# Block-quantised MLP of a two-layer decoder: down projection from float32r halves, split over two steps, block maxima kept in a PSUM bank

## The reference

```python
def _mx_dequant(t):                      # blocks of 32 along the last dim
    blocks = t.reshape(rows, feat // _BLOCK, _BLOCK)
    max_abs = jnp.max(jnp.abs(blocks), axis=-1)
    scales = jnp.maximum(max_abs / _FP8_MAX, _EPS)
    q = (blocks / scales[..., None]).astype(jnp.float8_e4m3fn).astype(jnp.float32)
    return (q * scales[..., None]).reshape(rows, feat)

def _mx_linear(x2d, w):
    return _mx_dequant(x2d) @ _mx_dequant(w).T
...
gate = _mx_linear(x2d, gate_w)
up = _mx_linear(x2d, up_w)
...
out = _mx_linear(h, down_w)
...
x = x + _L1_ffn_ref(_layernorm(x, axis=-1), L1_ffn_gate_w, L1_ffn_up_w, L1_ffn_down_w)
```

## Time and profile before

| | us |
|---|---|
| median of 3 runs | 1530.81 |
| the profiled execution | 1529.1 |
| its span in the profile | 1527.0 |
| TensorE busy | 1450.7 (95%) |
| VectorE busy | 1117.6 (73%) |
| ScalarE busy | 978.1 (64%) |
| GpSimd busy | 730.9 (48%) |
| the last stage, first projection to the end of the span | 1348.0 to 1527.0 |

### The profile page before, as it was taken

How to read it: one execution, slowest core, us unless ns; L and a number is a source line. 1 busy time by engine, 2 the same in 40 slices (tenths; PEclk the granted TensorE clock), 3 DMA queues, 4 the chain that set the end, 5 groups by cost and what they waited for, 6 DMA issues and landing times. The chain is left out here.

```text
span 1527.0 us, 30711 instructions
## 1 busy us (share of the span) xinstructions
PE 1450.7 (95%) x10384; PEld 1201.9 (79%) x10384; DVE 1117.6 (73%) x2544; ACT 978.1 (64%) x2620; POOL 730.9 (48%) x894
## 2 busy tenths in 40 slices
PE   5999899999999999899998999899999999889998
PEld 3676578888888888688874555489999999867887
DVE  5888678888888887554446777656777777788887
ACT  2787577777778777433336888677877777742222
POOL 3766545555555555232323343113444444457765
PEclk9999999999999999999999999999999999999999
DMA  6000010000000000000002000120000000000000
GB/s 255 2 2 2 29 69 3 5 3 5 3 3 5 4 3 1 24 1 1 1 20 119 2 1 2 33 80 8 8 8 9 8 2 2 1 1 15 14 11 18
DMA packets 15611, 29.84 MB, mean 20 GB/s; under 512 B 1505, under 2 KB 12002, under 8 KB 14690
## 3 DMA queue, kind: packets, MB, share of 16 engines
q1 hardware_dynamic: 15458, 27.89, 5.0%
HBM read 25.79 MB, written 2.10 MB: 18 GB/s over the span
## 5 line engine op out<-in xcount | busy, mean ns | idle before, releaser
L1517 POOL TENSOR_TENSOR weights_even<-weights_even,cross_reciprocal 128x512 f32<-128x512 f32 x64 | 66.6, 1040 | 189.1 <-DVE cross_reciprocal L1771 189.1
L962 POOL TENSOR_TENSOR cross_work<-cross_work,cross_reciprocal 128x512 f32<-128x512 f32 x64 | 66.6, 1040 | 175.2 <-DVE cross_reciprocal L1130 175.2
L1208 PE MATMUL bank<-ident,cross_work 128*128 128x128 f32 x768 | 116.9, 275 | 1.4 <-DVE cross_work L1108 1.1
L1015 ACT ACTIVATE cross_work<-bank,cross_shift,cross_q_rms 128x128 f32<-128x128 f32 x256 | 113.6, 455 | 4.5 <-DVE cross_shift L1102 3.5
L1208 PEld LDWEIGHTS bank<-ident,cross_work 128*128 128x128 f32 x768 | 89.5, 140 | 29.0 <-DVE cross_work L1108 20.5
L2062 POOL TENSOR_TENSOR mlp_low_inner<-mlp_inner,mlp_high_inner 128x512 fp32r<-128x512 f32 x35 | 47.5, 1356 | 114.5 <-ACT mlp_high_inner L2106 114.5
L2598 DVE TENSOR_REDUCE grouped_maxima<-bank 128x4 bf16<-128x512 f32 x128 | 82.3, 684 | 25.5 <-PE bank L2690 25.5
L1606 ACT ACTIVATE weights_even<-bank,cross_shift 128x128 f32<-128x128 f32 x256 | 90.4, 366 | 13.0 <-DVE cross_shift L1763 12.0
L1761 DVE TENSOR_REDUCE cross_maxima<-bank 128x4 f32<-128x512 f32 x64 | 44.1, 689 | 69.6 <-PE bank L1909 69.6
L2962 ACT ACTIVATE mx_silu<-bank 128x512 f32<-128x512 f32 x32 | 19.1, 598 | 113.4 <-PE bank L3112 113.3
L411 POOL TENSOR_TENSOR causal_masked_maxima<-causal_maxima,causal_constants 128x512 bf16<-128x512 bf16 x64 | 66.5, 1061 | 45.0 <-DVE causal_maxima L562 40.7
(11 more groups left out here) (388 smaller groups left out, 5357.4 us busy)
## 6 DMA issues: line engine op xcount, KB each, us to landing
weights_even<-in_weights SPq DMA_DIRECT2D x2, 2560.0 KB, 12.4
weights_even<-in_weights SPq DMA_DIRECT2D x2, 1732.0 KB, 9.6
weights_odd_early<-in_weights SPq DMA_DIRECT2D x1, 3072.0 KB, 11.8
weights_odd_values<-in_weights SPq DMA_DIRECT2D x1, 3072.0 KB, 18.9
weights_odd_late<-in_weights SPq DMA_DIRECT2D x2, 1536.0 KB, 9.5
x<-in_x SPq DMA_DIRECT2D x4, 512.0 KB, 8.2
out<-mx_result SPq DMA_DIRECT2D x16, 128.0 KB, 1.7
weights_even<-in_weights SPq DMA_DIRECT2D x2, 512.0 KB, 6.1
```

The costliest lines, as they stand in the source:

```text
L962: pool.tensor_tensor(probs[x], probs[x], reciprocal[x][:, :].unsqueeze(2).to_broadcast([P, PER, P]), ALU.mult).then_inc(probs_divided, 1)
L1015: last = act.activation(probs[x][:, j, :], bank_scores[:, j * P:(j + 1) * P], ACT.Exp, scale=q_rms[x][:, j:j + 1], bias=shift[x][:, j:j + ...
L1208: last = pe.transpose(bank[:, j * P:(j + 1) * P], source, core.ident[:, :])
L1517: pool.tensor_tensor(probs[x], probs[x], reciprocal[x][:, :].unsqueeze(2).to_broadcast([P, JOBS, P]), ALU.mult).then_inc(probs_divided, 1)
```

## The change

The down projection is made of float32r halves, as the up projection was already: `innerT` and the down weights each become a high and a low tensor, and for each tile three products of 128x256 are made (high with high weights, high with low weights, low with high weights), 24 for a batch. The high part of the transposed inner half is ScalarE's copy, as before, now with float32r out. The low part is new work of VectorE: `make_low_innerT`, PSUM minus high part, 128x512, one for each half, placed between `gate` and `scale_inner`. The low down weights are made once by GpSimd, four subtractions of 128x512 between the roundings of batch 0 (`low_down_weights`); ScalarE writes the high ones with four more copies.

Half 0 of a batch's down projection stays at its place at the end of step b+2 (`down_half(t - 2, 0)`). Half 1 is made one step later, behind the first projection of step b+3. So `bank_y` is complete one piece later, and `add_to_x` of batch t-3 moves behind `scale_inner` of half 0.

`largest` of the inner scaling is the first 16 columns of the bank of the up projection, which is free once `gate` has read it.

```diff
-        self.largest, self.scale, self.inverse = (layer.sbuf(f"{name}_{x}", [P, blocks])
-                                                  for x in ("largest", "scale", "inverse"))
+        self.largest = layer.sbuf(f"{name}_largest", [P, blocks]) if largest is None else largest
...
-        scratch = [Scratch(layer, f"inner{j}", INTER // HALVES) for j in range(HALVES)]
+        banks_of_up = [core.banks[2], core.banks[4]]
+        scratch = [Scratch(layer, f"inner{j}", INTER // HALVES, largest=banks_of_up[j][:, 0:INTER // HALVES // BLOCK])
+                   for j in range(HALVES)]
...
+            def low_down_weights(jobs):
+                for k in jobs:
+                    pool.wait_ge(weights_ready, GATE_UP_JOBS - TURNED_EARLY + k + 1)
+                    tiles = slice(2 * k, 2 * k + 2)
+                    pool.tensor_tensor(down_split[1][:, tiles, :], w_down[:, tiles, :],
+                                       down_split[0][:, tiles, :].bitcast(F32), ALU.subtract).then_inc(down_low, 1)
...
+                    if isinstance(b, int) and b == 0:
+                        low_down_weights((2 * j, 2 * j + 1))
...
+                        act.activation(down_split[0][:, m:m + 2, :].rearrange("p i n -> p (i n)"),
+                                       bank_turn[k % 2][:, :], ACT.Copy)
...
+            def make_low_innerT(b, j):
+                dve.wait_ge(innerT_high, HALVES * b + j + 1)
+                dve.tensor_tensor(innerT[1][:, 4 * j:4 * j + 4, :], bank_turn[j].rearrange("p (i t) -> p i t", i=4),
+                                  innerT[0][:, 4 * j:4 * j + 4, :].bitcast(F32), ALU.subtract).then_inc(innerT_low, 1)
...
-                if batch_there(t - 3) and t - 3 != VERY_LAST - 1:
+                if batch_there(t - 3) and not batch_there(t - 1) and t - 3 != VERY_LAST - 1:
                     add_to_x(t - 3, 1 - s)
...
                         if j == 1 and batch_there(t):
                             make_low(t)
+                        if batch_there(t - 2):
+                            make_low_innerT(t - 2, j)
                         scale_inner(i, j)
+                        if j == 0 and batch_there(t - 3):
+                            add_to_x(t - 3, 1 - s)
...
+            WITH_HIGH, WITH_LOW = ((0, 0), (0, 1)), ((1, 0),)
+
+            def down_half(b, j):
+                if j == 0:
+                    pe.wait_ge(result_ready, nonneg(b))
+                if isinstance(b, int) and b == 0:
+                    pe.wait_ge(down_low, (j + 1) * (WEIGHT_JOBS - GATE_UP_JOBS) // HALVES)
+                tiles = range(4 * j, 4 * j + 4)
+                pe.wait_ge(innerT_high, HALVES * b + j + 1)
+                down_products(tiles, WITH_HIGH, first=(j == 0))
+                pe.wait_ge(innerT_low, HALVES * b + j + 1)
+                product = down_products(tiles, WITH_LOW, last=(j == HALVES - 1))
+                if j == HALVES - 1:
+                    product.then_inc(layer.y_filled, 1)
...
                     if batch_there(t - 1):
                         project(t - 1, j)
+                    if j == 0 and batch_there(t - 3) and t - 3 != VERY_LAST:
+                        down_half(t - 3, 1)
                     if batch_there(t - 2):
                         turn_inner(t - 2, s, j)
...
-                    down(t - 2)
+                    down_half(t - 2, 0)
```

More of the change, by code:

```diff
@@ L2860, in mx_mlp @@
         inner_q = [sbuf(f"inner_q{s}", [P, INTER]) for s in range(2)]
-        innerT = sbuf("innerT", [P, TILES, P])
+        innerT = [sbuf(f"{half}_innerT", [P, TILES, P], F32R) for half in ("high", "low")]
+        down_split = [sbuf(f"{half}_down", [P, TILES, EMBED], F32R) for half in ("high", "low")]
         result = [sbuf(f"result{s}", [P, EMBED]) for s in range(2)]
         bank_h, bank_turn, bank_y = core.banks[0], core.banks[5:7], core.banks[7]
-        bank_gate, bank_up = [core.banks[1], core.banks[3]], [core.banks[2], core.banks[4]]
+        bank_gate, bank_up = [core.banks[1], core.banks[3]], banks_of_up
         weight_banks = [core.banks[k] for k in (5, 6, 7, 3)]
@@ L2991, in step @@
                     if batch_there(t - 2) and (t - 2, j) != (VERY_LAST, 1):
-                        copy_innerT(t - 2, j)
+                        copy_high_innerT(t - 2, j)
                 if t - 2 == VERY_LAST:
@@ L3084, in step @@
                     make_low(t)
+                if t - 2 == VERY_LAST:
+                    make_low_innerT(VERY_LAST, 0)
+                    for k in range(PIECES):
+                        make_low_last_piece(k)
             batches(dve, step)
@@ L3129, in turn_h, with down_products @@
                 last.then_inc(layer.hT_filled, 1)
-            def down(b):
-                pe.wait_ge(result_ready, nonneg(b))
-                for m in range(TILES):
-                    if m % 4 == 0:
-                        pe.wait_ge(innerT_ready, HALVES * b + m // 4 + 1)
-                    last = pe.matmul(bank_y[:, 0:EMBED], innerT[:, m, :], w_down[:, m, :],
-                                     start=(m == 0), stop=(m == TILES - 1))
-                last.then_inc(layer.y_filled, 1)
-            def down_tiles(tiles):
-                for m in tiles:
-                    last = pe.matmul(bank_y[:, 0:EMBED], innerT[:, m, :], w_down[:, m, :],
-                                     start=(m == 0), stop=(m == TILES - 1))
-                return last
+            def down_products(tiles, parts, first=False, last=False):
+                jobs = [(m, a, b) for m in tiles for a, b in parts]
+                for k, (m, a, b) in enumerate(jobs):
+                    product = pe.matmul(bank_y[:, 0:EMBED], innerT[a][:, m, :], down_split[b][:, m, :],
+                                        start=(first and k == 0), stop=(last and k == len(jobs) - 1))
+                return product
+            WITH_HIGH, WITH_LOW = ((0, 0), (0, 1)), ((1, 0),)
[11 more added lines that the diff above has]
+                    product.then_inc(layer.y_filled, 1)
             def last_batch(s):
@@ L3158, in turn_piece @@
                     last.then_inc(last_turned, 1)
+                down_half(VERY_LAST - 1, 1)
                 turn_inner(VERY_LAST, s, 0)
                 pe.wait_ge(result_ready, VERY_LAST)
-                pe.wait_ge(innerT_ready, HALVES * VERY_LAST + 1)
-                down_tiles(range(half // 2))
+                pe.wait_ge(innerT_high, HALVES * VERY_LAST + 1)
+                down_products(range(half), WITH_HIGH, first=True)
                 turn_piece(0)
-                down_tiles(range(half // 2, half))
+                pe.wait_ge(innerT_low, HALVES * VERY_LAST + 1)
+                down_products(range(half), WITH_LOW)
                 turn_piece(1)
                 for k in range(PIECES):
-                    pe.wait_ge(last_copied, k + 1)
-                    last = down_tiles(tiles_of(k))
-                last.then_inc(layer.y_filled, 1)
+                    pe.wait_ge(last_high, k + 1)
+                    down_products(tiles_of(k), WITH_HIGH)
+                    pe.wait_ge(last_low, k + 1)
+                    product = down_products(tiles_of(k), WITH_LOW, last=(k == PIECES - 1))
+                product.then_inc(layer.y_filled, 1)
             def step(t, s):
```

28 lines of the change are left out of this document (17 added, 11 removed).

## The result

The changed kernel takes **1545.68 us** (median of 4 runs, 1542.21 to 1546.94) against 1528.91 (4 runs, 1526.64 to 1532.58; the three runs shown ahead and one more): ratio 1.0101 (95% interval 1.0084 to 1.0118), slower by more than 0.5%, as forecast, and within the range. The profiled execution, against which the sum was made, took 1542.21 with a span of 1540.2; the forecast for it was 1541.5, and 1543 by the median.

What follows compares the result with a forecast made beforehand. TensorE was taken to bound the middle, VectorE and GpSimd the first batches; afterwards a loop through both TensorE and VectorE. Start +4.1, middle +5.9 and end +2.4 on 1529.1 gave 1541.5 us (1543 by the median), range 1534 to 1550.

Steps and rivals of the forecast that it cites:

- What bounds: Last stage before the change: VectorE and GpSimd set the first four batches' pace, TensorE the middle, at 10.26 us a step.
- TensorE alone, 9.63: Middle: with shorter down products and a first projection some 0.2 faster, TensorE alone would do a step in 9.63 us.
- Maxima: Inner scaling: L789 reading PSUM no longer waits for GpSimd, freeing VectorE of 1.2 us a step, without surcharge.
- The loop: Middle, from one addition's end to the next through TensorE, ScalarE's copy and VectorE: 10.80 us a step, +5.9 us.
- the handovers: In the loop, passing work between engines: 0.07 us for two with ScalarE's copy, 0.03 in VectorE's part.
- Start: First four batches: later make_low of batch 1, added low parts and port waits, less L789's gain: +4.1 us.
- the three port waits of 2.5: Start: VectorE's rounder operations wait for GpSimd's weight subtractions three times, 0.7 to 1 us each, 2.5 in all.
- End: Last batch: scaling waits 1.5 us for a low part, an addition adds 0.33, the last pieces 0.6; +2.4 us.
- Sum: Whole stage: 4.1 + 5.9 + 2.4 = +12.4 us on the profiled 1529.1, giving 1541.5 us.
- TensorE's pace: Rival, middle: the addition comes in time, step 9.63 us, time 1528.7, or 1524 or less; chance 0.16 together.
- The moved port wait: Rival, middle: L802 or L804 waits for GpSimd instead of L789, loop 0.72 us longer, time 1549.4; chance 0.08.

Runs made afterwards that it cites:

- E1: The changed kernel with make_low_innerT behind scale_inner instead of ahead of it, in both halves; 1529.52 us, ratio 0.9984.
- E4: The kernel before with only the maxima of the inner scaling moved to PSUM, the bank of the up projection; 1527.44 us, ratio 0.9981.
- E5: The changed kernel with VectorE's order scaling, addition, low part; 1529.41 us, ratio 0.9999.
- E2: The changed kernel with the addition to x between low part and scaling of half 0; 1540.67 us, ratio 1.0071.
- E7: The changed kernel with add_to_x at the start of VectorE's step, low part still ahead of the scaling; 1536.48 us, ratio 1.0048.
- E10: The changed kernel with ScalarE's copies for the high down weights moved behind its copy of h of batch 1; 1546.87 us, ratio 1.0097.
- E9: E5 with plain float32 down products for batch 0, batch 14's second half and batch 15, and E10's move; 1527.57 us, ratio 0.9990.
- E12: E1 with both halves of the down projection at the end of TensorE's step; 1577.25 us, ratio 1.0308.
- E11: E9 with batches 0 and 1 plain in the order of the kernel before, GpSimd's weight subtractions spread over both; 1526.11 us, ratio 0.9981.

## Why the prediction was right, point by point

**What bounds.** Right: TensorE was full before, and E1, E4 and E5 all stop where it is full again.

**TensorE alone, 9.63.** The floor is 9.73 in E1 and E5. The 0.10 more is the first projection, which got 0.09 faster behind the split products and not 0.2 (E5: 1406.20 - 1401.51 - 1.43 = 3.26 up to the second, for 1397.90 - 1394.55 = 3.35). The down products take what was forecast (1452.35 - 1450.81 = 1.54 for 1.52, 1.43 for 1.43).

**Maxima.** Right that L789 falls to 0.17 and that a PSUM source costs so small an operation nothing: 0.174 out of PSUM in every row, and the smallest out of SBUF is 0.174. The 62 cycles that the Trainium skill adds (VectorE: DVE Perf Modes, TRN2 errata), an estimate of 0.065 us, are not there. What the forecast missed is that the time which L789 gives back is not all VectorE's: in E4 two thirds of it come back on L802. In the changed kernel they do not, and then only because of where the scaling falls.

**The loop.** Shown, by moves at different places: E1 and E2 take the scaling out of it, E5 and E7 put the addition ahead of the wait for the copy, and the wait for the addition before L3169 goes in each. Forecast 10.80, measured 10.93. Term by term: TensorE 1.54 + 2.80 + 1.43 + 0.60 = 6.37 for 6.35; copy 0.60 for 0.59; VectorE from 1446.98 to 1450.34, with the addition 0.42, 3.78 for 3.76; the handovers 0.04, 0.10 and 0.05, together 0.19 for 0.10. The mis-sized term is the handovers, ScalarE to VectorE above all (0.10). So the middle gave +7.4 for +5.9.

**Start**, +4.1 forecast, +3.35 measured. `make_low` of batch 1 comes 1.60 later (1358.69 - 1347.83 = 10.86 for 1357.30 - 1348.04 = 9.26), forecast 1.5; from there to that of batch 3 it is 1385.80 - 1358.69 = 27.11, 1.87 more for 2.6; the rest 0.12 less. The term that was mis-sized is the three port waits of 2.5: the rows show three smaller ones, 0.81 and 0.67 on L802 for 0.43 and 1.25 on L804 of h for 0.29, so 0.38 + 0.24 + 0.96 = 1.6. The picture behind the sum held. The 1.60 are VectorE's wait for the copy of h (2.94 for 1.35), and between the two `make_low` it waits for the result of no other engine, while its busy time grows by the same 1.87 (25.94 for 24.07 us). E10 took the first of these away, and the start got no shorter.

**End**, +2.4 forecast, +2.67 measured; E9, which makes the end plain, has 19.67, so the split products and their low parts there are the whole of it. The terms came out, 1.62 for 1.5, 0.34 for 0.33 and 0.57 for 0.6. The sum left out the low part of batch 14's second half (0.61) and a longer L802 (0.24), and that L804's long wait of 0.72 would be gone; these nearly cancel.

**Sum.** 3.35 + 7.39 + 2.67 = 13.4 in the stage for 12.4. That it came so near is in part luck: the start was forecast 0.75 too high and the middle 1.45 too low. By the medians the change costs more (16.8, ratio 1.0084 to 1.0118, so 12.8 to 18.0): the profiled execution was the fastest of its four. The earlier stages, which the change doesn't touch, can differ by more than that from one execution to another: the first projection of batch 0 starts anywhere from 1345.19 to 1359.25 in the profiles of the kernels here.

**Rivals.** TensorE's pace was the alternative, and it decides on one line's place, as E1 shows; the point given for it (VectorE's part of the loop under 2.6 us) is in accord with E1, where the scaling is out of that part. The moved port wait was absent from the changed kernel's middle (L802 427 ns, L804 428), present in E2's (549), and large in E4's (812).

## What to carry to other kernels

When a transfer or conversion is added to an in-order queue, ask of each item behind it whether it needs it: put what waits for another engine's newest result last, and the release that another engine waits for first. Moves that only pay together (here a product postponed by a step, and the operation that feeds it behind the independent work) are costed together, for each of them alone can be slower than none. A gain in the steady part is read against the start and the end of the stage: here they ate 4.3 of 5.8 us.

## What was not expected

**TensorE's clock falls behind some of its idle stretches.** Busy time and granted clock (third from the end) of the start, before and then changed:

```profile
1350.00:1360.00 10.00, 8.42 (x45) 6.57 (x44) 7.46 (x16) 5.40 (x10) 3.59 (x3) 1.00 0.00 0
1360.00:1370.00 10.00, 8.41 (x42) 6.58 (x40) 9.52 (x18) 3.35 (x7) 6.42 (x7) 1.00 0.00 0
1370.00:1380.00 10.00, 8.41 (x41) 6.70 (x42) 9.56 (x17) 2.86 (x6) 8.07 (x8) 1.00 0.04 13
```

```profile
1350.00:1360.00 10.00, 6.99 (x37) 5.23 (x36) 5.91 (x15) 7.04 (x14) 4.55 (x4) 0.98 0.00 0
1360.00:1370.00 10.00, 9.37 (x45) 7.51 (x43) 9.62 (x15) 3.24 (x7) 8.94 (x9) 0.85 0.00 0
1370.00:1380.00 10.00, 7.19 (x32) 6.14 (x33) 9.55 (x18) 1.20 (x2) 7.89 (x8) 0.83 0.00 0
```

TensorE worked 6.99 of 10 us in the changed kernel and 8.42 before, waited 1.89 us for `make_low` right before 1359.17, and its clock then fell from 2.4 towards 1.2 GHz for a part of each of the next stretches. Every kernel with the split products has such a fall in the start, the kernel before and E4 have none; E5 has it in the end too, where a product takes 0.41 instead of 0.28 behind a wait of 2.07. What it costs depends on what stands beside it. In the changed kernel the slow products are in the projections at 1359.17 and 1372.81, where VectorE has work without a wait until 1389, so they cost the start little or nothing. In E10 (above) they are also in the projection of batch 3, which `gate` waits for, and cost some 1.4 us there (seven products at 0.43 for 0.23). No kernel here has the split products and an undisturbed clock. E12 has it in the middle, with the same two waits in each step (1.3 and 1.8) but a fall in only three of them, so what decides is more than the last wait; that stays open.

**An operation that loses its wait can hand it on.** E4 shows it without any other change: L789 loses 0.60 us a half (773 to 174 ns), L802 gains 0.39 (426 to 812). In the middle of the changed kernel, E1 and E5 the wait is nowhere (L802 427 to 428 ns). There the L802 of either half starts when GpSimd's last rounding operation is just ending or has ended: in the changed kernel at 1443.34 and 1449.54, with L811 ending at 1443.44 and 1448.11. In the start of E10 and E11 both L802 and L804 are longer (E11: 896 and 703 ns on average for 427 and 427 before), but there GpSimd also has the four weight subtractions, and the two causes are not set apart.
